# Row maxima in four steps over three PSUM banks, and a new order for the routing behind attention

## What is computed

```python
    dots = jnp.einsum('bhid,bhjd->bhij', q, k) * scale
    attn = jax.nn.softmax(dots, axis=-1)
    ...
    _, top_group_idx = jax.lax.top_k(group_scores, n_top_groups)
    ...
    top_scores, top_idx = jax.lax.top_k(masked, K)
    gates = jax.nn.softmax(top_scores, axis=-1)
    capacity = max(1, int(N / E * K * CAP_FACTOR))
    ...
    buf = jnp.zeros((E + 1, capacity, d), xf.dtype).at[e_s, p_s].set(xf[tok])[:E]
    h = jax.nn.silu(jnp.einsum('ecd,edh->ech', buf, wg)) * jnp.einsum('ecd,edh->ech', buf, wu)
    out_e = jnp.einsum('ech,ehd->ecd', h, wd)
    ...
    return (shared + routed).reshape(b, s, d)
```

## Time and profile before

| | us |
|---|---|
| median of three runs | 1708.82 |
| the profiled execution's own time | 1708.1 |
| span of its trace | 1706.4 |
| mean granted TensorE clock | 0.971 of full |
| busy: PE, DVE, POOL, ACT | 1520.7, 1053.5, 936.3, 797.0 |

### The profile page before, as it was taken

One profiled execution on the slowest core, in us unless ns is written; L12 is line 12 of the kernel. 1 busy time (PEld: TensorE's weight loads), 2 busy tenths in 40 slices (PEclk: granted clock), 3 DMA queues, 4 the chain that ended last, 5 costly groups with the idle time before them and its releaser, 6 DMA issues.

```text
span 1706.4 us, 24003 instructions
## 1 busy us (share of the span) xinstructions
PE 1520.7 (89%) x8086; PEld 1070.6 (63%) x8086; DVE 1053.5 (62%) x1770; ACT 797.0 (47%) x1501; POOL 936.3 (55%) x747
## 2 busy tenths in 40 slices
PE   3798999998989989899899998987789999999995
PEld 3465555555555556555565555544678999999995
DVE  6556666576565656667666676565645666666662
ACT  3344444444444435544354443444225566666663
POOL 4456666666565665666557677784432343333433
PEclk8899999999999999999999999998798999999998
DMA  3032440000000000000001010111225676666664
GB/s 99 12 77 68 89 97 10 23 14 10 14 10 23 14 10 23 14 10 14 10 23 30 26 31 23 30 45 56 72 92 176 171 196 166 184 181 167 192 170 93
DMA packets 99283, 117.94 MB, mean 69 GB/s; under 512 B 10595, under 2 KB 78181, under 8 KB 99173
## 3 DMA queue, kind: packets, MB, share of 16 engines
q1 hardware_dynamic: 82149, 96.97, 19.4%
q0 software_dynamic: 17056, 19.97, 6.0%
HBM read 74.93 MB, written 35.06 MB: 64 GB/s over the span
## 4 chain that ended last, share of the span: by engine, by line
PE 67%; DVE 17%; POOL 6%; ACT 6%; issue 2%; DMA 0%; SPq 0%; POOLq 0%; DVEq 0%; ACTq 0%
PE ps_o L921 10%; DVE piece_max L1279 9%; PE ps_t L780 9%; PE ps_m L780 8%; PE ps_m L883 8%; PE ps_st L780 8%; POOL arena L725 5%; PE ps_st L906 4%; PE ps_t L941 4%; PE ps_st L910 3%; PE ps_st L817 2%; PE ps_o L817 2%; ACT arena_r L1546 2%; PE ps_t L986 2%; PE ps_t L889 2%
## 5 line engine op out<-in xcount | busy, mean ns | idle before, releaser
L725 POOL TENSOR_TENSOR arena<-arena 128x512 f32<-128x512 f32 (+1 forms) x512 | 662.0, 1294 | 388.9 <-ACT arena L1569 350.7
L1569 ACT ACTIVATE arena<-ps_st 128x512 f32<-128x512 f32 (+1 forms) x576 | 328.0, 597 | 492.3 <-PE ps_st L910 473.2
L1279 DVE TENSOR_REDUCE piece_max<-ps_m 128x2 f32<-128x738 f32 x384 | 353.2, 920 | 223.9 <-PE ps_m L883 221.3
L755 POOL DMA_INDIRECT acc_rows<-arena,ids x96 | 150.7, 1570 | 291.2 <-ACT arena L1629 263.5
L883 PE MATMUL ps_m<-arena_r 128*128 128x370 f32 x768 | 220.4, 368 | 76.5 <-DVE piece_max L1279 69.9
L921 PE MATMUL ps_o<-arena 128*64 128x512 f32 (+1 forms) x1152 | 272.3, 608 | 0.0
L906 PE MATMUL ps_st<-arena_r 128*128 128x512 f32 (+1 forms) x576 | 242.1, 420 | 0.7 <-ACT arena L1569 0.7
L883 PEld LDWEIGHTS ps_m<-arena_r 128*128 128x128 f32 x768 | 130.2, 191 | 175.2 <-DVE piece_max L1279 148.6
L910 PE MATMUL ps_st<-arena_r 68*128 68x512 f32 (+2 forms) x576 | 229.7, 399 | 0.4 <-DVE arena_r L1292 0.4
L921 PEld LDWEIGHTS ps_o<-arena 128*64 128x64 f32 (+1 forms) x1152 | 75.1, 138 | 145.1 <-issue 138.1
L780 PE MATMUL ps_m<-arena_r 128*128 128x320 f32 (+1 forms) x864 | 163.9, 325 | 1.2 <-DVE arena_r L1431 1.2
(11 more groups left out here) (183 smaller groups left out, 1859.3 us busy)
## 6 DMA issues: line engine op xcount, KB each, us to landing
arena<-in_L_ffn_wg_dram SPq DMA_DIRECT2D x32, 512.0 KB, 4.5
arena<-in_L_ffn_wu_dram SPq DMA_DIRECT2D x32, 512.0 KB, 6.2
arena<-in_L_ffn_wd_dram SPq DMA_DIRECT2D x32, 512.0 KB, 4.0
x_slots<-route SPq DMA_DIRECT2D x5, 2176.0 KB, 12.9
arena<-x_slots SPq DMA_DIRECT2D x32, 272.0 KB, 2.7
arena_r<-arena_r SPq DMA_DIRECT2D x30, 275.2 KB, 4.0
arena<-in_L_xattn_Wkv_dram SPq DMA_DIRECT2D x32, 128.0 KB, 2.4
arena<-x_slots SPq DMA_DIRECT2D x32, 68.0 KB, 2.4
```

Source lines behind the costliest of these rows:

```text
L725: pool.tensor_tensor(total, probsT[0:rows, h, 0, :] if kt == 1 else total, probsT[0:rows, h, kt, :], ALU.add).then_inc(added, 1)
L755: pool.indirect_dma_start(out=dst[:, :], in_=y_sb[par][:, c, 0:w], in_offset=None, compute_op=ALU.add, out_offset=bass.IndirectOffsetOnAxi ...
L1279: dve.tensor_reduce(piece_max[:, :, :].rearrange("p a k -> p (a k)")[:, 2 * i:2 * i + 2], ps_m[:, :, 0:PIECE_W], AX.X, ALU.max).then_inc(m ...
L1569: act.activation(probsT[0:rows, h, kt, :], ps_st[0:rows, n % 3, :], ACT.Exp).then_inc(exp_done, 1)
```

## The change

- `ps_m` gets three banks and `ps_st` two. A `max` step is now three matmuls of 512, 512 and 78 columns over the three banks, and one DVE reduction of 128x1101 with negation straight into `neg`. There are four steps per half, no `piece_max` and no `neg` event. Where the steps stand in the slots is new. `exp_of` and `ps_st` go by 2 instead of 3.
- Routing jobs of groups 2 and 3 get a ring of their own: the third bank of `ps_m`, and `ps_o`. The experts' second result bank is the third bank of `ps_m`.
- The list of the tail is in another order, `lowh` of chunk 0 goes to POOL, and the loads and splits of the shared expert's weights stand at other slots of blocks 30 and 31. The last `out` stands right behind its first half.
- The rows of expert 0 are loaded by an event `feed` and transposed by `erow` ahead of the last `accout`; the pads are gone.

```diff
+        own_max = [own("max", d, 1, i) for i in range(4)]
+        next_max = [nxt("max", n, 0, i) for i in range(4)]
         out = [old("out", prev, i) for i in range(2)]
+        after = {(0, 8): [own("row", d, 1), old("sum", prev)],
                  (1, 1): [],
+                 (1, 2): [old("norm", prev), next_max[0]],
+                 (1, 3): first_values + [next_max[1]]}
         if project:
+            after[0, 0] = [own_max[0]] + project_k(0) + [own_max[1], k_low[0]]
             after[0, 2] = project_k(2) + [own_max[2], k_low[2]]
+            after[0, 3] = project_k(1) + [k_low[1]]
+            after[0, 5] = project_q() + [q_again] + last_values + [q_low, own_max[3]]
+            after[1, 4] = [out[0], next_max[2]]
+            after[1, 5] = [nxt("v", pp, 0), next_max[3]]
+            after[1, 6] = more_values + [nxt("row", n, 0), out[1]]
...
         else:
+            after[0, 0] = [own_max[0]] + project_q() + [own_max[1]]
+            after[0, 3] = [own_max[2]]
+            after[0, 5] = [q_again] + last_values + [q_low, own_max[3]]
+            after[1, 4] = [out[0], next_max[2]]
+            after[1, 6] = [out[1], next_max[3]] + more_values + [nxt("row", n, 0)]
...
+    tail = av + [("up", 0, 0), ("norm_a", 2), ("norm_b", 2), total, ("silu", 0, 0), ("hid", 0, 0), ("up", 0, 1),
+                 ("turned", 2, 0), ("turned", 2, 1), norm, ("silu", 0, 1), ("low", 2, 0), ("low", 2, 1), ("norm_c", 2),
+                 ("hid", 0, 1), ("up", 0, 2), ("score", 2)] + outs
+    tail += [("silu", 0, 2), ("high", 0, 0), ("lowh", 0, 0), ("scored", 2), ("hid", 0, 2), ("ws", 2), ("wl", 2),
+             ("stat_a", 3), ("stat_b", 3), ("up", 0, 3), ("root", 3), ("high", 0, 1), ("lowh", 0, 1), ("top", 2),
+             ("silu", 0, 3), ("high", 0, 2), ("lowh", 0, 2), ("hid", 0, 3), ("mask_a", 2), ("mask_b", 2),
+             ("high", 0, 3), ("lowh", 0, 3), ("best_a", 2), ("best_b", 2), ("down", 0), ("accout", 0), ("up", 1, 0),
+             ("norm_a", 3), ("norm_b", 3), ("silu", 1, 0), ("hid", 1, 0), ("turned", 3, 0), ("turned", 3, 1),
...
+    tail += hidden(2, 0) + hidden(2, 1) + [("pos", 3), ("gates", 3), ("places_a", 3), ("places_b", 3)] + scats[3]
+    tail += hidden(2, 2) + hidden(2, 3) + last(2)
...
+    tail += last(3)[:-1] + [("feed",), ("erow", 0), ("erow", 1)] + last(3)[-1:]
...
-        ps_m = stack.enter_context(nc.psum_tensor("ps_m", [P, 2, 512], F32))
-        ps_st = stack.enter_context(nc.psum_tensor("ps_st", [P, 3, 512], F32))
+        ps_m = stack.enter_context(nc.psum_tensor("ps_m", [P, 3, 512], F32))
+        ps_st = stack.enter_context(nc.psum_tensor("ps_st", [P, 2, 512], F32))
+        route_bank = (ps_m[:, 2, :], ps_o[:, :])
...
+                if kind == "lowh" and ev[1] == 0:
+                    ht = ev[2]
+                    pool.wait_ge(hid_hi_done, ht + 1)
+                    pool.tensor_tensor(hid_lo[:, ht, :], hid32[ht][:, :], hid_hi[:, ht, :].bitcast(F32), ALU.subtract)\
...
-                    pe.wait_ge(max_done, T * MAX_T + (d * 2 + h) * MAX_STEPS + i + 1)
-                    for bank_m, piece in enumerate((2 * i, 2 * i + 1)):
-                        c = d % 2 * 512 + piece // KEY_PIECES * P
-                        lo = piece % KEY_PIECES * PIECE
+                    pe.wait_ge(max_done, T * MAX_T + d * 8 + h * 4 + i + 1)
+                    c = d % 2 * 512 + i * P
+                    for lo, w in ((0, 512), (512, 512), (S, CT + 1)):
+                        mm = pe.matmul(scores_m[:, lo:lo + w], q1[h][:, c:c + P], k1[pp][h][:, lo:lo + w],
...
+                    dve.tensor_reduce(neg[h][:, c:c + 1], scores_m[:, 0:KEYS], AX.X, ALU.max, negate=True)\
+                       .then_inc(max_done, 1)
```

More of the change, by code:

```diff
@@ L232, in whole_plan @@
                 plan += [(new, T) for at, new in more if at == place]
-                if 0 <= T - back < TURNS:
+                late = (ev, T - back) == (("out", LAST_D - 1, 1), LAST_T)
+                if 0 <= T - back < TURNS and not late:
                     plan.append((ev, T - back))
+                    if (ev, T - back) == (("out", LAST_D - 1, 0), LAST_T):
+                        plan.append((("out", LAST_D - 1, 1), LAST_T))
                 elif T == 0 and ev[0] == "out":
@@ L249, in last @@
         return [("high", c, HIDS - 1), ("lowh", c, HIDS - 1), ("down", c), ("accout", c)]
[L251 to L259, removed]
@@ new lines, in whole_plan @@
+    tail += [("silu", 1, 2), ("high", 1, 1), ("hid", 1, 2), ("lowh", 1, 1), ("up", 1, 3), ("scored", 3), ("top", 3),
+             ("silu", 1, 3), ("high", 1, 2), ("hid", 1, 3), ("lowh", 1, 2), ("mask_a", 3), ("mask_b", 3),
+             ("best_a", 3), ("best_b", 3)] + last(1) + [("hot_a", 3), ("hot_b", 3), ("hot_c", 3), ("gexp", 3)]
+    tail += hidden(2, 0) + hidden(2, 1) + [("pos", 3), ("gates", 3), ("places_a", 3), ("places_b", 3)] + scats[3]
+    tail += hidden(2, 2) + hidden(2, 3) + last(2)
@@ L264, in whole_plan @@
     for ht in range(HIDS):
         tail += hidden(3, ht) + ([("ws1", ht)] if ht < WPIECES else [])
-    tail += last(3)
+    tail += last(3)[:-1] + [("feed",), ("erow", 0), ("erow", 1)] + last(3)[-1:]
     return plan + [(ev, LAST_T) for ev in tail]
-JOB_KINDS = ("k", "q", "v", "row", "sum", "out", "cen", "zt", "turned", "score", "pos")
+ROUTE_KINDS = ("turned", "score", "pos")
+JOB_KINDS = ("k", "q", "v", "row", "sum", "out", "cen", "zt", "erow") + ROUTE_KINDS
 def xattn_moe(nc, x, ctx_in, ln_m_g, ln_m_b, ln_l_g, ln_l_b, Wq, Wkv, Wout, group_c, expert_c, e_bias,
@@ L969, in _ @@
                        lambda k: hT_lo[:, k, a * 512:(a + 1) * 512], a * HT)
+                if kind == "erow":
+                    if a == 0:
+                        pe.wait_ge(rows_in[0], 48)
+                    for c, (lo, rows) in enumerate(CAP_TILES):
+                        mm = pe.transpose(bank[:, lo:lo + rows], xg[0][0:rows, c, a * P:(a + 1) * P], ident[0:rows, 0:rows])
+                    mm.then_inc(ready_of(jn), 1)
                 if kind == "down":
@@ L1203, in _ @@
                     jn = JOB[ev, T]
-                    bank, free = ps_t[jn % 2], job_free[jn % 2]
+                    bank, free = bank_of(jn), free_of(jn)
                 if kind == "kv":
@@ L1379, in _ @@
                        .then_inc(gu_free, 1)
-                if kind == "lowh":
+                if kind == "lowh" and a:
                     low_hid(a * HT + ev[2])
```

208 lines of the change are left out of this document (94 added, 114 removed).

## The result

| | before | after |
|---|---|---|
| median, us | 1708.69 (4 runs) | 1655.86 (4 runs, 1654.41 to 1659.20) |
| ratio | | 0.9696, 95% interval 0.9675 to 0.9717 |
| the profiled execution's own time | 1708.1 | 1654.7 |
| span of its trace | 1706.4 | 1653.0 |
| mean granted clock | 0.971 | 0.977 |

The kernel is faster by 3%, inside the range of the prediction, but by 53 us where 71 were forecast. The last three lines add up to the span: attention gave 37.4 of the 47 forecast for it and the start, the tail 14.9 and the experts' start 1.0 of the 24.

The account below looks back on a forecast made before the run. PE sets the pace, and its waits, chiefly for maximum reductions, are nearly all the rest. 1708.1 less 46 (attention), 1 (start) and 24 (tail) gives 1637 us; range 1610 to 1671.

Parts of the forecast that it names:

- The narrow matmul at 0.11: Maximum step: the 78-column matmul costs PE 0.11 us, bound by the 128x128 weight load, making a step 0.57.
- The bank wait: Scores with two banks: where three `st` stand together, the third waits for the exponential, 0.54 us lost each time.
- The walk through the unit: Attention, four parts of a unit: gains of 2.05, 0.85 and 0.8 and a loss of 0.3, together 3.4 us.
- the one by which the bank wait eats the gain: Rival: 10 slots a unit lose another 0.2 us each, attention gives 14 us, time 1669; chance 0.12.
- the slower one: Rival: exponentials queue behind ACT's copies at 4 places a unit, up to 2.4 us each, time 1791; chance 0.03.
- The narrow matmul at 0.23: Rival, maximum step: +0.12 x 256 = 31 us, half under waits, time 1652, in the forecast's range; no chance given.
- the tail gives little: Rival: POOL's `lowh` and scatters bind; `down` 0 and the rows come 8 us later, 16 of 24 go, 1653; chance 0.10.
- I take 0.5 a unit off: Attention: POOL's scatters delaying `norm` and `out`, and routing steps on DVE, reduce the gain to 2.9 us a unit.
- The last unit: End of attention: counted like every other of the 16 units, 2.9 us each; 5.8 for the two before first `up`.
- 3.4 us of 69.0 a unit: Attention: gain of one unit against its old time, 609.66 less 540.67, before 0.5 is taken off.
- some 97 us behind the first `up`: Tail: the first expert starts then instead of 119.7; with 1 to 2 us at the experts' start, 24 us gained.
- `row`'s wait about as before: Attention, sign to look for: PE's wait at `row` for the last maxima, 18.1 us in 33 waits before, stays.

Follow-up runs that it names:

- experiment 5: Kernel after the change, with the 78-column matmul of every maximum step issued twice: 1674.10 us, ratio 0.9798 to the kernel before.
- experiment 1: Kernel before the change, with scores using two PSUM banks in turn instead of three: 1728.09 us, ratio 1.0106.
- experiment 6: Kernel after the change, with `lowh` of chunk 0 on DVE instead of POOL: 1653.15 us, ratio 0.9671 to the kernel before.
- experiment 4: Kernel after the change, with the four `zs` events moved from between the first two maximum steps to slot (0, 4) of the next block: 1649.78 us.
- Experiment 7: Kernel after the change, with `high` and `lowh` of chunk 1's last quarter ahead of `mask` and `best` of group 3: 1649.87 us, ratio 0.9649.
- Experiment 2: Kernel after the change, with the old order of the tail and `lowh` of chunk 0 back on DVE: 1662.61 us, ratio 0.9727.

## Why the prediction was right, and where it was not

**Right.** The cause and the sign: idle time of PE behind reductions turned into work. The reduction at 1.30 us, three banks at no extra price, in 256 instructions. The narrow matmul at 0.11, by two views: the starts in the unit and experiment 5. The isolated-matmul formula of the Trainium skill (TensorE: Matmul & The Clock Gate, Back-to-back issue gap) gives 35 ns for it. The same section says that this formula under-counts small matmuls in a stream of weight loads and matmuls, and this case's trace agrees: 0.10 to 0.11 us. The price does not go by columns between 40 and 128 (0.107 and 0.106). That it is the load of the 128x128 weights is my reading; no run varied the weights. The bank wait: 88 waits of 0.31 where 80 to 100 of 0.3 to 0.5 were named, and 0.53 for a place of three where undoing it showed. The walk through the unit: 65.3 in an undisturbed one against 65.55 (66.3 in the one shown). The waits that the new tail would have at `down` 0 and `down` 1, the end of `down` 0, and the scatters that end just ahead of the row load. Of the rivals, the one by which the bank wait eats the gain is refuted by the waits and experiment 1, and so is the slower one: 88 waits on exponentials, the longest 1.0 us. The narrow matmul at 0.23 is refuted by experiment 5. Half of what the rival "the tail gives little" names did come, 8 of its 16 us, but not by its mechanism: the scatters ended 97.5 us behind the first `up` instead of near 89, yet PE waited only 0.65 for the rows, and experiment 6 took `lowh` off POOL for nothing.

The total is inside the range partly by the range's width: attention gave 37.4 of 47 and the tail 16 of 24, both less than forecast, both within their stated bounds.

**Wrong, the terms of the sum.**
- *"I take 0.5 a unit off" for POOL's and DVE's other work.* The disturbances were named, but as an average, and mis-sized: 1.15 a unit in rows 12 to 28 and 0.8 in rows 36 to 56, over the 0.4 by which an undisturbed unit falls short. The walk asked whether POOL fits in and put the long reciprocal right. It did not ask what the routing's 2.66 us does in the one place where it now stands between two reductions; experiment 4 undid this for 5.3 us. That the steps of blocks 18 to 27, and the split in block 28, cost the rest in the same way is read from the trace and was not tried. The old cycle forgave such an instruction: the same work cost it 0.1 there.
- *The last unit.* 5.8 forecast, -1.4 measured. The walk was made for a repeating unit and multiplied by 16, though this one has no `q` to put between steps 0 and 1. The bare wait of 1.40 is 0.5 us dearer than the old order's part (14.77 against 14.24); through the clock it became 3.2, and slow passes of the last `out` cost 1.6 more.
- *"3.4 us of 69.0 a unit".* The walk was right, its base was not. An undisturbed unit takes 65.3 us, where the walk gave 65.55, but it took 68.3 and not 69.0 before: the unit of the earlier trace rows has the split on DVE in its first half, which costs 0.6 in the old order and 1.05 in the new one. So the walk, made without the split, was set against a unit with it, and the gain is 3.0. Four of the 16 units have the split.
- *The tail: "some 97 us behind the first `up`", with a clock of 0.9 or more.* It was 104.8 at a clock of 0.80 and 0.87. The terms named do not add up to 97: 119.7 less the 26 gone, plus new waits of 6 and 4 and 3 of slow passes, is 107, near what came. The 97 stands beside a walk of the scatters (89) and of `down` 3 (92), and both were too fast: they ended 97.5 and 101.7 behind the first `up`. I gave `down` 0 a slow stretch of "perhaps 3 us", and it ended when forecast; `down` 1 I gave none. The waits were about as long as forecast, 5.4 and 4.2 us, but they came in six pieces with slow passes between and behind them. Experiment 7 shows the size: with a wait nearly as long in `down` 1 but no slow passes behind it, 2.9 us come back. Experiment 2 shows that of the 15 us only 7 were the order's.
- *"`row`'s wait about as before".* It fell from 18.1 to 3.0: the bank wait in front of `row` gives DVE the time. I had used this very overlap for the sum and not for the sign to look for.

What stays open is why the clock falls at one wait of 1.4 us and not at another: the waits of 1.45 before 477.64 and of 1.58 before 1014.68 left it alone. Episodes stood at different rows in kernels whose order is the same there, so part of the difference between any two single traces here, 1.5 to 3 us each time, is theirs.

## What to carry to other kernels

Fewer and longer reductions pay when PE waits for each, but the slack between them goes: list every instruction that the reducing engine runs between two of them, and move it before counting the gain. When a ring loses a bank, count the places where its users stand in rows longer than the ring, and put a piece of other work between them; some are hidden behind another wait. When you walk a stretch in the new order, take its old time from a stretch with the same side work. In a stretch where PE has little slack, price each short wait with the clock that may follow it.

## What the runs showed of the hardware

- Half-clock episodes in the middle of a busy stream. The ten traces, cut by rows, had from one to six each, the first two parts and the last left out, and each cost 1.4 to 3.1 us. They began behind waits such as 1.40 and 0.39 within 4 us (after, at 1095.79), or 0.40, 0.55 and 0.56 within 4 us (before, at 475.12: a maximum step's record is 0.99 us long where one behind such a wait has 0.61). Three such waits (0.54, 0.56 and 0.56 within 4 us) at 545.59 to 548.84 in the same trace left the clock alone. In the 40 us around the one at 475, PE was 92% busy at a granted clock of 0.91:
```profile
455.00:495.00 40.00, 36.90 (x163) 22.22 (x162) 23.00 (x27) 16.10 (x29) 24.28 (x19) 0.91 0.04 11
```
- A matmul's cost need not appear in its own row: of the 0.11 us of the narrow one, 0.08 show in the distance of the two passes behind it. With 128x128 weights, matmuls of 40, 78 and 128 columns all cost 0.10 to 0.11.
- A reduction over three PSUM banks in one instruction runs at the same 1.04 ns an element as one over two (1299 ns for 1101, 920 for 738).
